# Preparing the ternary weights of an FFN inside the attention that runs before it

## Chip, cores and metric

One core of a Trainium2 chip runs the whole program as one launch. The metric is the device time of that launch in microseconds. The kernel before takes 2642.88 us as the median of three runs (2640.75 to 2642.96).

## What is computed

Two decoder layers over x of 8 batch elements x 256 tokens x 512. Each layer is a gated cross-attention and a gated FFN. The change concerns the first attention (16 heads of 32, with RMS-normed q and k) and the first FFN, a quantised one. Cut to its core:

```python
def activation_quant(x):                      # 8 bits, a scale per token
    s = 127 / clip(max(abs(x), axis=-1, keepdims=True), 1e-5)
    return clip(round(x * s), -128, 127) / s
def weight_quant(w):                          # ternary, one scale per matrix
    s = 1.0 / clip(mean(abs(w)), 1e-5)
    return clip(round(w * s), -1.0, 1.0) / s
def bit_linear(x, w):
    return einsum('bsh,oh->bso', activation_quant(x), weight_quant(w))
# x += tanh(g0) * attention(layernorm(x), context)
# n = layernorm(x);  h = silu(bit_linear(n, w_gate)) * bit_linear(n, w_up)
# x += tanh(g_ffn0) * bit_linear(rms_norm(h) * ln_weight, w_down)
```

Each of the three weight matrices has 512 x 2048 fp32 elements, 8192 on each of 128 partitions (4 MB). The mean of the magnitudes runs over the whole matrix, so no element can be rounded before all of its matrix have been summed.

## The kernel before

The program is written by hand in five parts that run one after another: `image_attention` (tag a), `quantised_ffn` (tag b), `cross_attention`, `latent_attention` and `expert_ffn`. The residual x stays in SBUF all the time as `x_res`, 16 tiles of 128 tokens x 512 fp32, two tiles for each batch element. Within a part every engine has its own instruction list and waits on semaphores; there is no planner.

**The first attention.** The loop runs over turns i from -2 to 7. Turn i finishes batch element i (exponentials, weighting of the values, output projection, addition to x) and starts element i + 1 (values, queries, their norms, transposes, scores) and the keys of i + 2. The order of each engine within a turn is written out: TensorE L592 to L658, ScalarE L739 to L776, VectorE L898 to L948, POOL L440 to L452. ScalarE makes in each turn: the turned peaks (`peaks`, L672), the high half of the turned x (`x_high`), exponentials of four groups of heads, squares of keys and queries with a sum, the high half of the context, high halves of keys and queries, and a copy and a high half of the outputs (`output_raw`, `output_high`). Each fp32 product is made of three products of high and low halves (`split_product`, L45). Products go through a ring of three PSUM banks; `use_of` (L350) numbers their uses in order, and a use waits until the use three before it has been read. `add_to_x` (L878, an addition at L882) is VectorE's last work of a turn. Weights of the attention are held as `w_hi` and `w_lo`, four tensors each; that of the output is `WO`. SP's queue loads x in three transfers (the last is 3 MB, L383) and one context for each turn (L386), the latter once POOL has read the one before (`ctx_lo_done`). `spread` (L791) takes the layer norm's statistics of an element before it is used. POOL begins with memsets (L416 to L420) and selections (L426, L431); ScalarE's first instruction (L730) waits for these.

**The quantised FFN** has a preparation with a block of its own (L976 to L1034). SP loads the three raw matrices (4 MB each), the gate and the layer norm's row. For each matrix ScalarE sums magnitudes (L997), TensorE adds the partitions by a product with ones (L1018), VectorE makes mean and inverse (L1028, L1030), scales and clips in two passes over the 8192 columns (L1032, L1034) and ScalarE rounds to bf16 (L1001). VectorE also takes the statistics of all 16 tiles (L106), aggregates them (L109) and makes an inverse root (L112, L79 to L86). Then a second block holds the FFN proper: its VectorE list begins with the gain product (L1298), which is followed by the norm, the rounding of x and its transposes; the first matmuls are at L1101.

Of the kernel before, what the change touches and what calls it, by code (L numbers as in the profile page):

```python
# [21 lines left out]
P = 128  # L22
# [69 lines left out]
class Norm:  # L92


    def __init__(self, nc, tag, x, begun, place):
        self.x, self.begun = x, begun
        self.stats, self.agg, self.var, self.rstd, self.tmp = (
            place(nc.sbuf_tensor(f"{tag}_ln_{n}", [P, TILES, *shape], F32))
            for n, shape in (("stats", (6,)), ("agg", (2,)), ("var", ()), ("rstd", ()), ("tmp", ())))
        self.stats_done, self.steps = nc.alloc_semaphore(f"{tag}_ln_stats_done"), nc.alloc_semaphore(f"{tag}_ln_steps")  # L100

    def find_spread(self, dve, chain, first, end):

        part = slice(first, end)
        with dve.Fori(first, end) as n:
            dve.bn_stats(self.stats[:, bass.ds(n, 1), :].rearrange("p o n -> p (o n)"), tile_of(self.x, n)).then_inc(self.stats_done, 1)  # L106
        dve.wait_ge(self.stats_done, end)
# [163 lines left out]
def image_attention(nc, x_res, ident, begun, x_in, ctx_t, w_t, rows, gate):  # L271
# [14 lines left out]
    CHAIN = 1 + 9  # L286

    with ExitStack() as ctx:
# [6 lines left out]
        w_hi = [sb(f"w_hi{n}", [P, C, D], F32R) for n in range(4)]  # L295
        w_lo = [sb(f"w_lo{n}", [P, C, D], F32R) for n in range(4)]
# [29 lines left out]
        x_in0, x_in1, x_rest, ctx_in = sem("x_in0"), sem("x_in1"), sem("x_rest"), sem("ctx_in")  # L326
# [24 lines left out]
        for i in TURNS:  # L351
            for name, ahead in PLACES:
                if here(i + ahead) and (name, i + ahead) not in use_of:
                    use_of[name, i + ahead] = len(use_of)

# [13 lines left out]
        def _(sp):  # L369
            sp.dma_start(x_res[:, 0:TB, :], x_in[:, 0:TB, :]).then_inc(x_in0, 16)  # L370
# [8 lines left out]
            sp.dma_start(x_res[:, TB:2 * TB, :], x_in[:, TB:2 * TB, :]).then_inc(x_in1, 16)  # L379
# [3 lines left out]
            sp.dma_start(x_res[:, 2 * TB:, :], x_in[:, 2 * TB:, :]).then_inc(x_rest, 16)  # L383
            for s in range(1, BATCH):
                sp.wait_ge(ctx_lo_done, s)
                sp.dma_start(ctx_f[:, :, :], ctx_t[s]).then_inc(ctx_in, 16)  # L386

        @block.gpsimd
        def _(pool):
# [26 lines left out]
            pool.memset(eps[:, :], RMS_EPS).then_inc(eps_done, 1)  # L416
            pool.memset(neg_peak[:, :, :], 0.0).then_inc(blanked, 1)
# [37 lines left out]
        def _(pe):  # L455
# [130 lines left out]

            pe.wait_ge(begun, 1)
# [2608 lines left out]
```

## Time and profile before

| | before |
|---|---|
| median of 3 runs (lowest, highest) | 2642.88 us (2640.75, 2642.96) |
| the profiled execution: its time, its span | 2643.05 us, 2641.3 us |
| TensorE matmul busy (share of the span) | 2247.1 us (85%) |
| VectorE busy | 1411.7 us (53%) |
| ScalarE busy | 957.3 us (36%) |
| POOL busy | 826.5 us (31%) |
| DMA | 166.46 MB, mean 63 GB/s |

The span is the time from the first to the last recorded instruction of the profiled execution; its own time, 1.75 us longer, is what stands beside the median. Busy times are averages over five parts with different limits, so a stretch has to be read by itself. "PEclk" is the granted clock of TensorE as a share of 2.4 GHz. In the timelines the number in brackets is the idle time of the engine before an instruction, and behind the arrow stands what ended it. A line is that of the kernel before.

### The profile page before, as it was taken

To read this page: it belongs to the slowest core of one execution; us is meant where nothing else is said; L and a number is where in the kernel's file an instruction comes from. 1 tells how busy PE (TensorE), PEld (TensorE's weight loads), DVE (VectorE), ACT (ScalarE), POOL (GpSimd) and SP (SyncE) were. 2 spreads that over 40 slices of the span, in tenths; PEclk is the share of its full clock that TensorE was granted. 3 is DMA by queue.
4 is the path that set the end of the run, shared out by engine and by line. 5 is a ranking of instruction groups with operands and counts; after the bars stand their busy time and mean duration, and the time that the engine had idled before them with its cause. 6 is when DMAs were issued, how large, how long until landed. Compare 5 with 4: busy or idle time off the path is not lost. (4 is left out here: it accounts for less than half of the span.)

```text
span 2641.3 us, 44093 instructions
## 1 busy us (share of the span) xinstructions
PE 2247.1 (85%) x17154; PEld 1824.4 (69%) x17154; DVE 1411.7 (53%) x2430; ACT 957.3 (36%) x1683; POOL 826.5 (31%) x736
## 2 busy tenths in 40 slices
PE   6989984277756999899989998999679999689995
PEld 4666663133325998799879997999556676579995
DVE  7787774677774333433343334333354444567776
ACT  2333332755533222322232222222244544325552
POOL 3332422033322232223222231222343544114543
PEclk8999997699987999999999998999879999899998
DMA  4000003100004001100110011100100000226775
GB/s 175 17 9 9 9 1 135 72 1 0 0 0 176 32 32 64 65 32 32 64 65 32 32 64 62 35 32 32 47 1 2 1 2 2 89 90 246 281 263 215
DMA packets 35814, 166.46 MB, mean 63 GB/s; under 512 B 5712, under 2 KB 5712, under 8 KB 29392
## 3 DMA queue, kind: packets, MB, share of 16 engines
q1 hardware_dynamic: 28624, 141.23, 14.3%
q0 software_dynamic: 7040, 23.07, 2.5%
q8 instruction: 113, 1.85, 0.3%
q14 instruction: 37, 0.30, 0.0%
HBM read 140.17 MB, written 24.12 MB: 62 GB/s over the span
## 5 line engine op out<-in xcount | busy, mean ns | idle before, releaser
L220 POOL TENSOR_TENSOR c_prob<-c_prob,c_inv_mass 128x512 f32<-128x512 f32 x128 | 130.4, 1040 | 392.7 <-DVE c_inv_mass L212 392.7
L202 ACT ACTIVATE c_prob<-c_s_ps,c_neg_peak 128x256 f32<-128x256 f32 x256 | 117.8, 472 | 343.8 <-DVE c_neg_peak L191 343.8
L47 PE MATMUL c_ring<-c_xt_lo,c_w_hi 128*128 128x256 f32 x512 | 149.4, 292 | 21.4 <-DVE c_w_lo L1641 18.7
L1485 POOL TENSOR_TENSOR c_ctx_lo<-c_ctx_f,c_ctx_hi 128x1024 fp32r<-128x1024 f32 x33 | 80.4, 2437 | 271.4 <-ACT c_ctx_hi L1590 271.4
L1074 POOL TENSOR_TENSOR b_hw<-b_h,b_lnw 128x512 f32<-128x512 f32 x64 | 80.1, 1272 | 251.2 <-DVE b_h L1236 251.2
L47 PE MATMUL c_ring<-c_ctx_lo,c_w_hi 128*128 128x256 f32 x512 | 146.6, 286 | 2.1 <-DVE c_qt L1637 2.1
L49 PE MATMUL c_ring<-c_xt_hi,c_w_lo 128*128 128x256 f32 x512 | 143.9, 281 | 0.0
L49 PE MATMUL c_ring<-c_ctx_hi,c_w_lo 128*128 128x256 f32 x512 | 143.8, 281 | 0.0
L48 PE MATMUL c_ring<-c_xt_hi,c_w_hi 128*128 128x256 f32 x512 | 143.7, 281 | 0.0
L48 PE MATMUL c_ring<-c_ctx_hi,c_w_hi 128*128 128x256 f32 x512 | 143.6, 280 | 0.0
L1481 POOL TENSOR_TENSOR c_xt_lo<-c_xt_f,c_xt_hi 128x1024 fp32r<-128x1024 f32 x33 | 84.6, 2564 | 153.7 <-ACT c_xt_hi L1584 153.7
L176 PE MATMUL c_s_ps<-c_kt,c_qt 128*128 128x256 f32 x512 | 121.9, 381 | 8.5 <-ACT c_prob L202 4.8
L259 PE MATMUL c_o_ps<-c_prob_t,c_v 128*128 128x256 f32 x512 | 124.9, 400 | 4.4 <-DVE c_prob_t L247 4.4
L409 POOL TENSOR_TENSOR a_fold<-a_prob 128x1024 f32<-128x1024 f32 x32 | 76.2, 2383 | 147.5 <-ACT a_prob L715 145.8
L1682 DVE SCALAR_TENSOR_TENSOR x_res<-c_ring,c_gain,x_res 128x512 f32 (+1 forms) x64 | 48.1, 751 | 132.2 <-PE c_ring L49 132.2
L259 PEld LDWEIGHTS c_o_ps<-c_prob_t,c_v 128*128 128x128 f32 x512 | 103.1, 202 | 22.1 <-DVE c_prob_t L247 5.4
L47 PE MATMUL c_ring<-c_w_lo,c_o_hi 128*128 128x512 f32 x256 | 104.5, 408 | 10.3 <-DVE c_o_lo L268 7.9
L47 PEld LDWEIGHTS c_ring<-c_xt_lo,c_w_hi 128*128 128x128 f32 x512 | 96.7, 189 | 23.6 <-issue 20.3
L268 DVE TENSOR_TENSOR c_o_lo<-c_o_ps,c_o_hi 128x1024 fp32r<-128x1024 f32 x32 | 39.2, 1224 | 135.7 <-ACT c_o_hi L264 135.7
L176 PEld LDWEIGHTS c_s_ps<-c_kt,c_qt 128*128 128x128 f32 x512 | 94.0, 189 | 24.9 <-ACT c_prob L202 7.1
L1637 DVE COPY c_kt<-c_ring 128x512 f32<-128x512 f32 x64 | 44.3, 691 | 124.8 <-PE c_ring L49 124.8
L1637 DVE COPY c_qt<-c_ring 128x512 f32<-128x512 f32 x64 | 44.2, 691 | 124.1 <-PE c_ring L49 124.1
(514 smaller groups left out, 7119.3 us busy)
## 6 DMA issues: line engine op xcount, KB each, us to landing
e_raw<-e_w SPq DMA_DIRECT2D x16, 1536.0 KB, 6.4
c_xt_f<-xnt_scratch SPq DMA_DIRECT2D x33, 512.0 KB, 3.3
c_ctx_f<-ctx_t SPq DMA_DIRECT2D x33, 512.0 KB, 3.4
c_raw<-c_w SPq DMA_DIRECT2D x16, 1024.0 KB, 6.2
b_raw<-b_w SPq DMA_DIRECT2D x3, 4096.0 KB, 22.5
h_res<-e_w SPq DMA_DIRECT2D x8, 1536.0 KB
h_res<-pairs_scratch SPq DMA_DIRECT2D x10, 512.0 KB, 8.2
a_ctx_f<-ctx_t SPq DMA_DIRECT2D x8, 512.0 KB, 3.4
```

Source lines behind the costliest of these rows:

```text
L47: pe.matmul(out, lhs[0], rhs[1], start=first, stop=False)
L48: pe.matmul(out, lhs[0], rhs[0], start=False, stop=False)
L49: return pe.matmul(out, lhs[1], rhs[0], start=False, stop=last)
L176: mm = pe.matmul(self.s_ps[:, j, 0:w], q_of(u, j), k_of(u, j)[:, 0:w], start=mask is None, stop=True, skip_group_check=mask is not None)
L202: ins = act.activation(self.prob[:, u % 2, j, 0:w], self.s_ps[:, j, 0:w], ACT.Exp, bias=self.neg_peak[:, u % 2, j:j + 1], scale=self.scale ...
L220: pool.tensor_tensor(part, part, self.inv_mass[:, u % 2, js].unsqueeze(2).to_broadcast([P, 2, w]), ALU.mult).then_inc(self.prob_done, 1)
L259: mm = pe.matmul(out_of(g, j), v_of(g, j, t), self.prob_t[:, buf, t, j, :], start=(t == 0), stop=(t == TB - 1))
L409: pool.tensor_tensor(fold[:, n % 2], prob[:, n % 2, :, 0, :], prob[:, n % 2, :, 1, :], ALU.add).then_inc(fold_done, 1)
L1074: pool.tensor_tensor(hw[:, par, cols], h[:, par, cols], lnw[:, cols], ALU.mult).then_inc(hw_done, 1)
L1481: pool.tensor_tensor(xt_lo[:, :, :], xt_f[:, :, :], f32(xt_hi[:, :, :]), ALU.subtract).then_inc(xt_lo_done, 1)
L1485: pool.tensor_tensor(ctx_lo[:, :, :], ctx_f[:, :, :], f32(ctx_hi[:, :, :]), ALU.subtract).then_inc(ctx_lo_done, 1)
L1637: dve.tensor_copy(to, ring[:, k % 2, :]).then_inc(ring_free, count)
```

## The change

The three matrices are made ternary in the first attention. They come in pieces of 128 x 1024 fp32, eight for each matrix, 24 in all, twice: the 24 first steps sum magnitudes (one activation with a sum each), the 24 others round (Identity with the scale 1/mean and a shift of 12582912, then Sign of that less the shift, to bf16). Both are ScalarE's. The pieces lie in the tiles of x of elements 4 to 7, which are loaded later; rounded pieces are stored to DRAM and come back in three 2 MB loads into the place of the attention's q, k and v weights once their last product has been made. The number of steps at each of five places of ScalarE's turn is written out. The mean of all three matrices is one product and three VectorE instructions in turn 1. The layer norm statistics of the FFN are taken in the attention, one element per turn, one turn later, and the preparation block goes. Its DMAs of gate and row, Tanh, the bf16 identity, the aggregation and the root move to the head of the FFN proper.

```diff
 class Norm:
+        self.stats = stats if self.given else place(nc.sbuf_tensor(f"{tag}_ln_stats", [P, TILES, 6], F32))
     def find_spread(self, dve, chain, first, end):
-        with dve.Fori(first, end) as n:
-            dve.bn_stats(...)
-        dve.wait_ge(self.stats_done, end)
+        if not self.given:
+            with dve.Fori(first, end) as n:
+                dve.bn_stats(...)
+            dve.wait_ge(self.stats_done, end)
+PER_WEIGHT = 8
+class Handed:
+    def __init__(self, nc, ctx, w_dram):
+        self.wq = ctx.enter_context(nc.sbuf_tensor("ab_wq", [P, 3 * 2 * C * D], F32R))
+        self.w_mean = ctx.enter_context(nc.sbuf_tensor("ab_w_mean", [P, 3], F32))
+        self.stats = ctx.enter_context(nc.sbuf_tensor("ab_stats", [P, TILES, 6], F32))
+        self.w_dram = w_dram
+        self.wq_dram = nc.dram_tensor("wq_scratch", (3, P, PER_WEIGHT * 1024), BF16, kind="Internal").ap()
 def image_attention(...)
+    PIECE = 1024
+    PIECES = 3 * PER_WEIGHT
+    PLACES_OF_STEPS = {-1: (0, 2, 1, 1, 2), 0: (2, 4, 2, 4, 6), 1: (1, 2, 1, 3, 4), 2: (1, 2, 1, 2, 3), 3: (0, 1, 0, 1, 2)}
+        w_hi = [handed_part(2 * n) for n in range(3)] + [sb("w_hi3", [P, C, D], F32R)]
+        w_lo = [handed_part(2 * n + 1) for n in range(3)] + [sb("w_lo3", [P, C, D], F32R)]
         for i in TURNS:
+            if i == 1:
+                use_of["mean", 0] = len(use_of)
+        for i, n in STEPS.items():
+            for p in range(n):
+                r = p % 4 if i < 2 else (1 + p % 3 if i == 2 else 2 + p % 2)
+                buffer_of.append(r)
...
         @block.sync
-            sp.dma_start(x_res[:, 2 * TB:, :], x_in[:, 2 * TB:, :]).then_inc(x_rest, 16)
-            for s in range(1, BATCH):
+            sp.dma_start(x_res[:, 2 * TB:4 * TB, :], x_dram[:, 2 * TB:4 * TB, :]).then_inc(x_rest, 16)
+            def load_context(s):
                 sp.wait_ge(ctx_lo_done, s)
                 sp.dma_start(ctx_f[:, :, :], ctx_t[s]).then_inc(ctx_in, 16)
+            def load_piece(k):
+                r, n = buffer_of[k], k % PIECES
+                earlier = [j for j in range(k) if buffer_of[j] == r]
+                if earlier and earlier[-1] < PIECES:
+                    sp.wait_ge(summed, earlier[-1] + 1)
+                elif earlier:
+                    sp.wait_ge(piece_out[r], 16 * len([j for j in earlier if j >= PIECES]))
+                sp.dma_start(piece(k), handed.w_dram[n // PER_WEIGHT][:, cols]).then_inc(piece_in[r], 16)
+            def store_piece(k):
+                sp.wait_ge(rounded, n + 1)
+                sp.dma_start(handed.wq_dram[n // PER_WEIGHT][:, cols], piece(k).bitcast(BF16)[:, 0:PIECE]).then_inc(piece_out[buffer_of[k]], 16)
+            def load_late_x(s):
+                r = s - 4
+                sp.wait_ge(piece_out[r], 16 * len([j for j in range(PIECES, 2 * PIECES) if buffer_of[j] == r]))
+                sp.dma_start(x_res[:, s * TB:(s + 1) * TB, :], x_dram[:, s * TB:(s + 1) * TB, :]).then_inc(x_in[r], 16)
+            load_context(1)
+            for i in STEPS:
+                first = FIRST_STEP[i]
+                for p in range(STEPS[i]):
+                    k = first + p
+                    if i < 3:
+                        load_piece(k)
+                    if k - PIECES >= 2 and p >= 2:
+                        store_piece(k - 2)
+                    if i == 3:
+                        load_piece(k)
+                    if p == STEPS[i] // 2:
+                        load_context(i + 3)
+                if first + STEPS[i] > PIECES:
+                    store_piece(first + STEPS[i] - 2)
+                    store_piece(first + STEPS[i] - 1)
+                if i in (1, 2):
+                    load_late_x(i + 3)
+            load_late_x(6)
+            load_late_x(7)
+            load_context(7)
+            await_ready(sp, "q1", BATCH - 1)
+            for n in range(3):
+                sp.dma_start(handed.wq[...].bitcast(BF16), handed.wq_dram[n]).then_inc(wq_in, 16)
+            sp.wait_ge(wq_in, 48)
         @block.gpsimd
             pool.memset(eps[:, :], RMS_EPS).then_inc(eps_done, 1)
+            pool.memset(ones[:, :], 1.0)
+            pool.memset(shifts[:, 0:1], ROUND)
+            pool.memset(shifts[:, 1:2], -ROUND).then_inc(consts_done, 1)
         @block.tensor
                 if now:
                     turn_peaks(i)
+                if i == 1:
+                    use("mean", 0, mean)
                 if i >= 0 and nxt:
                     turn_x(i + 1, 0)
         @block.scalar
+            def next_weights(i, place):
+                for k in steps_of(i, place):
+                    await_piece(act, k)
+                    of = piece(k)
+                    if k < PIECES:
+                        if k > 0:
+                            act.wait_ge(summed, k)
+                        act.activation(of, of, ACT.Abs, accum_out=part[:, k:k + 1]).then_inc(summed, 1)
+                    else:
+                        n = k - PIECES
+                        w = n // PER_WEIGHT
+                        if n == 0:
+                            act.wait_ge(mean_steps, 3)
+                        act.activation(of, of, ACT.Identity, bias=shifts[:, 0:1], scale=inv_mean[:, w:w + 1]).then_inc(shifted, 1)
+                        act.wait_ge(shifted, n + 1)
+                        act.activation(of.bitcast(BF16)[:, 0:PIECE], of, ACT.Sign, bias=shifts[:, 1:2]).then_inc(rounded, 1)
                 if now:
                     exponentials(i, 0)
+                next_weights(i, 0)
...
                 if i >= -1 and here(i + 2):
                     context_high(i + 2)
+                next_weights(i, 1)
...
                     keys_high(i + 1, 1)
+                next_weights(i, 2)
...
                     output_raw(i, 1)
+                next_weights(i, 3)
                 if now:
                     output_high(i, 1)
+                next_weights(i, 4)
         @block.vector
+            def find_spread_after(i):
+                await_free(dve, "o1", i)
+                for t in range(TB):
+                    dve.bn_stats(handed.stats[:, i * TB + t, :], x_res[:, i * TB + t, :])
                     low("xt", i + 1, 0, xt_lo, xt_hi, xt_hi_done)
+                if i == 1:
+                    mean_magnitudes()
                 if nxt:
                     find_spread(i + 2)
+                if i >= 1:
+                    find_spread_after(i - 1)
+                if nxt:
                     value(i + 1, 0)
...
+            find_spread_after(BATCH - 1)
 def quantised_ffn(...)
-        with ExitStack() as prep:
...
+        @block.sync
+            sp.dma_start(gate_sb[:, :], gate).then_inc(gate_in, 16)
+            sp.dma_start(lnw[:, :], ln_row).then_inc(lnw_in, 16)
         @block.gpsimd
+            pool.wait_ge(lnw_in, 16)
             weight(0, 0)
         @block.scalar
+            act.wait_ge(gate_in, 16)
+            act.activation(gain[:, :], gate_sb[:, :], ACT.Tanh).then_inc(gain_done, 1)
             round_x(0)
         @block.vector
+            dve.tensor_copy(ident_b[:, :], ident[:, :])
+            norm_of.find_spread(dve, Chain(dve, norm_of.steps, begun), 0, TILES)
             chain.turn(0)
+            dve.wait_ge(gain_done, 1)
```

## Rows read from the trace of the kernel before

**Rows 1.** Windows: us, busy PE, PEld, DVE, ACT, POOL (instructions), PEclk, DMA share, GB/s
```profile
113.55:162.76 49.21, 45.09 (x452) 32.08 (x451) 38.69 (x56) 17.48 (x29) 16.95 (x9) 0.97 0.04 12
440.25:502.43 62.18, 1.73 (x6) 1.51 (x6) 40.64 (x58) 42.33 (x10) 0.00 (x0) 0.52 0.52 219
507.20:513.10 5.90, 4.72 (x17) 2.08 (x18) 0.00 (x0) 2.73 (x4) 0.00 (x0) 0.50 0.00 0
```

**Rows 2.** Timeline of VectorE, 438 to 503: start, duration, instruction, idle before
```profile
438.34 0.75 DVE L882 SCALAR_TENSOR_TENSOR x_res<-a_ring,a_gain,x_res 128x512 f32<-128x512 f32 x1 [2.05 <-PE a_ring L49]
440.25 0.17 DVE L1022 MEMSET b_ones<- 128x128 f32 x1 [1.16 <-PEq L3115]
...
440.57 9.59 DVE L106 BATCH_NORM_STATS2 b_ln_stats<-x_res  x16
450.19 1.17 DVE L109 BATCH_NORM_AGGREGATE b_ln_agg<-b_ln_stats 128x2 f32<-128x6 f32 x16
...
453.49 0.17 DVE L86 SCALAR_TENSOR_TENSOR b_ln_rstd<-b_ln_tmp,b_ln_rstd 128x16 f32<-128x16 f32 x1
...
502.43 0.21 DVE L1298 TENSOR_SCALAR b_down_gain<-b_w_mean,b_gain 128x1 f32<-128x1 f32 x1 [7.67 <-PEq L976]
```

**Rows 3.** DMA issues: count, KB each, median us to landing
```profile
b_raw<-b_w SPq DMA_DIRECT2D x3, 4096.0 KB, 22.5
...
h_res<-pairs_scratch SPq DMA_DIRECT2D x10, 512.0 KB, 8.2
a_ctx_f<-ctx_t SPq DMA_DIRECT2D x8, 512.0 KB, 3.4
...
out<-x_res SPq DMA_DIRECT2D x16, 256.0 KB, 2.4
...
c_gate_sb<-g_xattn SPq DMA_DIRECT2D x1, 0.5 KB, 2.0
```

**Rows 4.** Timeline of ScalarE: turn 1, a table load, two two-operand activations
```profile
120.06 0.60 ACT L682 ACTIVATE a_xt_hi<-a_ring 128x512 fp32r<-128x512 f32 x1 [2.77 <-PE a_ring L466]
120.55 0.62 ACT L698 ACTIVATE a_junk<-a_kf 128x512 bf16<-128x512 f32 x1
...
121.35 0.63 ACT L698 ACTIVATE a_junk<-a_kf 128x512 bf16<-128x512 f32 x1
...
124.11 1.06 ACT L670 ACTIVATE a_ctx_hi<-a_ctx_f 128x1024 fp32r<-128x1024 f32 x1 [0.21 <-PE a_ring L49]
130.57 0.63 ACT L705 ACTIVATE a_junk<-a_qf 128x512 bf16<-128x512 f32 x1 [5.39 <-DVE a_qf L842]
...
142.57 0.60 ACT L690 ACTIVATE a_qt_hi<-a_ring 128x512 fp32r<-128x512 f32 x1 [3.85 <-PE a_ring L466]
...
153.50 0.63 ACT L727 ACTIVATE a_o_hi<-a_o_f 128x512 fp32r<-128x512 f32 x1 [6.53 <-DVE a_o_f L875]
162.76 0.38 ACT L676 ACTIVATE a_peak_t<-a_ring 128x256 fp32r<-128x256 f32 x1 [8.63 <-PE a_ring L507]
...
511.39 1.28 ACT L1163 ACT_TABLE_LOAD   x1 [2.03 <-PE b_g_ps L1101]
...
1896.22 1.52 ACT L2145 ACTIVATE h_res<-x_res,d_shift,d_rstd 128x512 f32<-128x512 f32 x2 [1.43 <-DVE d_ratio L2312]
```

**Rows 5.** Timeline of VectorE, start of turn 1
```profile
113.34 0.75 DVE L882 SCALAR_TENSOR_TENSOR x_res<-a_ring,a_gain,x_res 128x512 f32<-128x512 f32 x1 [0.67 <-PE a_ring L49]
...
118.33 0.69 DVE L842 TENSOR_TENSOR a_v<-a_ring,a_row 128x512 f32<-128x512 f32 x1 [1.54 <-PE a_ring L49]
120.69 0.69 DVE L856 TENSOR_TENSOR a_xt_lo<-a_ring,a_xt_hi 128x512 fp32r<-128x512 f32 x1 [1.67 <-ACT a_xt_hi L682]
```

**Rows 6.** Timeline of ScalarE, start of the kernel
```profile
1.85 1.28 ACT L730 ACT_TABLE_LOAD   x1 [1.85 <-PEq L3108]
7.71 0.63 ACT L730 ACTIVATE a_pick<-a_fold 128x512 fp32r<-128x512 f32 x1 [4.58 <-POOL a_fold L426]
...
31.46 1.06 ACT L670 ACTIVATE a_ctx_hi<-a_ctx_f 128x1024 fp32r<-128x1024 f32 x1 [4.44 <-DMA a_ctx_f<-ctx_t]
```

More of the change, by code:

```diff
@@ L268, in output_low, with image_attention @@
         dve.tensor_tensor(to, of, f32(high), ALU.subtract).then_inc(self.o_lo_done, 1)
-def image_attention(nc, x_res, ident, begun, x_in, ctx_t, w_t, rows, gate):
+def image_attention(nc, x_res, ident, begun, x_dram, ctx_t, w_t, rows, gate, handed):
     tag = "a"
@@ L286, in image_attention @@
     CHAIN = 1 + 9
+    PIECE = 1024
+    PIECES = 3 * PER_WEIGHT
+    PLACES_OF_STEPS = {-1: (0, 2, 1, 1, 2), 0: (2, 4, 2, 4, 6), 1: (1, 2, 1, 3, 4), 2: (1, 2, 1, 2, 3), 3: (0, 1, 0, 1, 2)}
+    STEPS = {i: sum(n) for i, n in PLACES_OF_STEPS.items()}
+    FIRST_STEP = {i: sum(n for j, n in STEPS.items() if j < i) for i in STEPS}
     with ExitStack() as ctx:
@@ L354, in image_attention, with piece, await_piece, steps_of @@
                     use_of[name, i + ahead] = len(use_of)
+        buffer_of, users, later = [], [0] * 4, []
+        for i, n in STEPS.items():
+            for p in range(n):
+                r = p % 4 if i < 2 else (1 + p % 3 if i == 2 else 2 + p % 2)
+                buffer_of.append(r)
+                later.append(users[r])
+                users[r] += 1
+        def piece(k):
+            at = 2 * TB * TB + TB * buffer_of[k]
+            return x_res[:, at:at + TB, :].rearrange("p t d -> p (t d)")
+        def await_piece(eng, k):
+            eng.wait_ge(piece_in[buffer_of[k]], 16 * later[k] + 16)
+        def steps_of(i, place):
+            if i not in STEPS:
+                return range(0)
+            first = FIRST_STEP[i] + sum(PLACES_OF_STEPS[i][:place])
+            return range(first, first + PLACES_OF_STEPS[i][place])
         def bank_of(name, s):
@@ L585, in outputs, with mean @@
                 use(f"o{t}", i, projected(o_hi, o_lo, WO, t))
+            def mean(bank):
+                pe.wait_ge(consts_done, 1)
+                pe.wait_ge(summed, PIECES)
+                return pe.matmul(bank[:, 0:PIECES], ones[:, :], part[:, :], start=True, stop=True)
             pe.wait_ge(begun, 1)
@@ L775, in _ @@
                     output_raw(i, 1)
+                next_weights(i, 3)
+                if now:
                     output_high(i, 1)
+                next_weights(i, 4)
         @block.vector
@@ L948, in _, with quantised_ffn @@
                     add_to_x(i, 1)
-def quantised_ffn(nc, x_res, ident, begun, w_dram, ln_row, gate):
+            find_spread_after(BATCH - 1)
+def quantised_ffn(nc, x_res, ident, begun, handed, ln_row, gate):
     F = 2048
@@ L966, in sem @@
             return nc.alloc_semaphore(f"b_{name}")
-        wq = [sb(f"wq{n}", [P, WEIGHTS // P], BF16) for n in range(3)]
-        w_mean = sb("w_mean", [P, 3])
+        w_mean = handed.w_mean
         gate_sb, gain = sb("gate_sb", [P, 1]), sb("gain", [P, 1])
```

113 lines of the change are left out of this document (42 added, 71 removed).

## Prediction

> **What bounds the kernel now.** I read the busy time by stretch first. A steady turn of the first attention takes 49.2 us; TensorE is busy for 45.1 of them and ScalarE for 17.5 [rows 1]. So TensorE with its waits sets the turn and ScalarE is idle two thirds of it. From 440.25 to 502.43 the second program prepares its weights: 62.2 us in which TensorE works 1.7 and no DMA, VectorE or ScalarE work of any other stage goes on. Everything in it is on the path, because the first matmul of the FFN needs it. Next VectorE's order of time around that stretch [rows 2]: the last addition to x ends at 439.09, the first instruction of the next program comes at 440.25, sixteen statistics take 9.59, sixteen aggregates and the inverse root go from 450.19 to 453.66, and the gain product that opens the FFN proper starts at 502.43. Between 453.66 and 502.43 lies nothing but the weights, which have to land first (4 MB each, 22.5 us median, [rows 3]). The rows that are still needed afterwards are the aggregates and the root, 3.47 us.
>
> **What the change removes.** After the change VectorE leaves the attention 1.3 us later, since the two statistics of the last batch element come behind its last addition (the same instructions are 9.59/16 = 0.6 apart, [rows 2], with 0.1 for the end of the last). The change of programs costs 1.16 as now. Then the bf16 identity (0.1), aggregates and root (3.47): 439.09 + 1.3 + 1.16 + 0.1 + 3.47 = 445.1. The gain product now waits also for Tanh of the gate. Its DMA is SP's first of the stage; a load of that size lands in 2.0 [rows 3], issued near 441.5 with half a us of issue, so 444.0, Tanh 0.2: 1 us before VectorE asks. The ternary weights are in SBUF already: their load waits for the last q projection, which comes within turn 6, and turn 6 ends by 113.6 + 6 x 49.2 = 409. The second of the 4 MB loads landed after 22.5 with 8.4 MB moved, 370 GB/s, so 6.3 MB need 17: 426 at the latest, 13 us ahead, and more by what of turn 6 is left at its issue. If that cover went, up to 17 would stand on the path. The row of the layer norm (1 MB) has some 15 us before POOL reads it. So the FFN proper starts at 445.1 in place of 502.43: **57.3 us less**. A second effect I put at zero: the first matmuls run at a granted clock of 0.50, the 1.2 GHz level, in 507.2 to 513.1 after TensorE's idle time [rows 1]. Now its idle time shrinks by 57; if the clock stayed at 2.4 GHz, the 4.7 busy us of that stretch would take half, 2.4 less. Bounds: a gain of 2.4 or nothing.
>
> **What it adds on ScalarE.** There are 48 steps in turns -1 to 3. Price [rows 4]: a 128x1024 activation from SBUF takes 1.06; two with a sum (512 wide) start 0.80 apart, so a magnitude step of 1024 takes 0.80 + 0.43 = 1.23. A rounding step has Identity with two per-partition operands: two 512 wide with two such operands took 1.52 together, so 0.80 each with 0.08 of overlap, against 0.63 with none, so 1.06 + 0.17 = 1.23, then a wait for itself (0.08) and Sign with one operand (1.15), less overlap: 2.4. In all 24 x 1.23 + 24 x 2.4 = 87 us, set into the places of a turn where ScalarE waits. These five waits, in turn 1: 2.77, 5.39, 3.85, 6.53, 8.63 [rows 4]. Turn 0 has 2, 4, 2, 4, 6 magnitude steps: 2.5, 4.9, 2.5, 4.9, 7.4, all within. Turn 1 has 1, 2, 1, 3, 4 rounding steps: 2.4, 4.8, 2.4, 7.2, 9.6: the last two are over by 0.7 and 1.0. Behind the first stands the high half of the output, then POOL's low half, for which TensorE already waits; behind the second the turned peaks, for which TensorE waits too. Both are paid: **1.7**. Turn 2 (1, 2, 1, 2, 3) and turn 3 (0, 1, 0, 1, 2) fit.
>
> **The ring and the statistics.** In turn 1 the mean's product takes a bank of the ring between the turned peaks and the first turned x. With three banks that x then needs the bank of the last output product, whose addition ends at 113.34 + 0.75 = 114.09 [rows 5], where it now starts at about 113.4: **0.7**, once. VectorE's statistics (1.3 each turn) and the mean's three small steps (0.6, turn 1) stand before the first value tile, where VectorE idles 1.54, and 1.67 before the next [rows 5]: nothing, or 0.3 in each of seven turns if the cover is short (2 us, upper bound).
>
> **SP's queue.** It now holds 24 loads twice, 24 stores, the split x and the contexts in one order. A 512 KB load lands in 3.4, a 256 KB store in 2.4 [rows 3]. In turn 1 a piece's load is issued when the piece three before it is rounded: lead two steps, 4.8, against 0.4 issue + 3.4: on time by 1. In turn 2 x of element 4 comes only after the last store of turn 1, 4 us late into the turn, which VectorE meets 2 us early; 1.3 + 1.6 of the idle times above absorb that. The piece behind it in the queue lands near 5.2 after the last rounding, ScalarE wants it at 4.1 and had 0.4 to spare: **0.8**. Later turns ask for x near 48 us after the buffer is free. Bounds for all of SP's effects: 0 and, if each piece lands as late as the slowest row of that size, 8.2 [rows 3], the rival below.
>
> **The start.** Three more memsets on POOL come before those that ScalarE's first instruction waits for (idle 4.58, released by POOL, [rows 6]); a memset of 128x128, the largest of them, took 0.17 [rows 2], so **0.3** for the three. In turn -1 the second context had waited 4.44 for its DMA behind 3 MB of x [rows 6]; now 2 MB fewer stand ahead, so it comes up to 3 us sooner and the two magnitude steps behind it fall into that time. Net nothing, with 2 us either way.
>
> **Sum.** 57.3 - 1.7 - 0.7 - 0.8 - 0.3 = 53.8 less. The profiled execution took 2643.05 (span 2641.3), the median of the runs is 2642.88; from either it comes to 2589.
>
> **Rivals.** (a) *Pieces come late.* With landings of 8.2 the lead of 4.8 is short by 3.8 and three steps take 8.2 + 0.5 + 2.4 = 11.1 in place of 7.2, 1.3 a step: up to 31 us over 24 rounding steps, of which the waits of the turn hide part. Say 10 to 28 more, 2599 to 2617. For it: two or three buffers only in turns 2 and 3, stores and loads in one order. Against it: DMA engines are 4% busy in these turns [rows 1]. 0.12.
> (b) *The steps are paid in full, slower than before.* A step that starts in a wait holds ScalarE's queue, and exponentials, copies and squares stand behind it. If nothing of the 87 us is hidden the time is 2589 + 87 - 1.7 = 2674. The kernel gets slower from 55 us on, that is where over 63% of the steps' time falls on the path: each place would have to start late by two thirds of its steps. The five waits of turn 1 sum to 27 us against 26.4 of steps, so turn 1 has no reserve, but turns 0, 2 and 3 have. 0.03.
> (c) *Sign needs another activation table than Exp.* No row has a Sign. One table load takes 1.28 where the trace has it [rows 4]; with one before and one after each Sign a rounding step takes 4.97, and against the same five waits turns 1, 2 and 3 run over by 27.5, 17.6 and 1.3, 46.4 in place of 1.7: 2634, still faster. Abs, Copy, Square, Exp and Tanh share a table here, as ScalarE loads one at 1.85 and the next at 511.39 [rows 4, 6]. 0.04.
> The Trainium skill, "ScalarE: Activation LUTs", section "What ACT_TABLE_LOAD costs", speaks against this change more strongly: each switch costs about 2.66 us with its drain. By that price a step would take 7.7 and the sum would come to 2698, slower than before. The same page's section on table sets names relu, copy, identity and abs as present in every set, and not Sign.
> (d) *Better than the sum:* the clock stays up at the FFN's start (2.4) and the small delays are covered by VectorE's waits: 2585 or 2586. 0.10.
>
> **The numbers.** The forecast has 0.71, its own range 2585 to 2594; (a) 0.12, (d) 0.10, (c) 0.04, (b) 0.03. The predicted time is the forecast's, 2589. The range of 8 in 10 takes in (d) and the lower part of (a): 2584 to 2603. About 0.2% (5.3 us) can be told from no change: faster 0.96, within 0.01 (what lies between (c) and (b)), slower 0.03 (b).
>
> **What would show it.** In the new profile: the gain product of the FFN near 502.4 - 53.8 = 448.6; no stretch of over 10 us with TensorE idle but the change of programs; turn 0 as long as before, turn 1 longer by about 2.4, turn 2 by about 0.8, turns 3 to 6 unchanged; ScalarE's waits at its five places nearly gone in turns 0 and 1, and waits "until DMA" there under 1 us; no table load in the attention but the first; the last load of ternary weights landing before 400. I am wrong if turns 1 to 3 grow by over 8 us together, if ScalarE waits for pieces by several us each, or if VectorE at the FFN's start waits for something not in my list.

## The result and the profile after

The changed kernel takes 2597.36 us (median of 4 runs, 2594.69 to 2599.41) against 2642.79 for the kernel before: a ratio of 0.9829 with a 95% interval of 0.9812 to 0.9846, 45 us faster. The forecast was 2589, its range of 8 in 10 2584 to 2603. The sign came out, 45 of the 54 us came out, and so did the mechanism; 8 us did not. The profiled execution is the 2599.41 one, the slowest of the four (span 2597.6). Its first attention opens as before and ends 10 us later; its FFN starts 46.5 us earlier.

VectorE at the change of programs, in the timeline of the changed kernel (start, duration, instruction, idle time before), answers to [rows 2]:

```profile
448.74 0.75 DVE L1023 SCALAR_TENSOR_TENSOR x_res<-a_ring,a_gain,x_res 128x512 f32<-128x512 f32 x1 [2.31 <-PE a_ring L49]
449.53 1.29 DVE L1029 BATCH_NORM_STATS2 ab_stats<-x_res 128x6 f32<-128x512 f32 x2
452.31 0.23 DVE L1403 CAST b_ident_b<-ident 128x128 bf16<-128x128 f32 x1 [1.49 <-PEq L3226]
452.45 1.16 DVE L111 BATCH_NORM_AGGREGATE b_ln_agg<-ab_stats 128x2 f32<-128x6 f32 x16
...
455.74 0.17 DVE L86 SCALAR_TENSOR_TENSOR b_ln_rstd<-b_ln_tmp,b_ln_rstd 128x16 f32<-128x16 f32 x1
455.94 0.21 DVE L1407 TENSOR_SCALAR b_down_gain<-ab_w_mean,b_gain 128x1 f32<-128x1 f32 x1
```

From the end of the last addition (449.49) to the gain product (455.94) is 6.45 us; it was 502.43 - 439.09 = 63.34 [rows 2]. The head alone gives 56.9.

Turns 1, 2 and 3 of the changed attention and the FFN's first matmuls, windows (busy PE, PEld, DVE, ACT, POOL, PEclk, DMA share, GB/s), to be held against the first and third of [rows 1]. A turn runs from the start of the turned peaks on ScalarE to the next:

```profile
113.16:166.27 53.11, 45.57 (x454) 32.33 (x454) 40.26 (x61) 42.55 (x50) 16.95 (x9) 0.97 0.51 167
166.27:218.29 52.02, 47.69 (x450) 34.56 (x450) 39.55 (x57) 38.00 (x48) 16.97 (x9) 0.90 0.51 157
218.29:269.26 50.97, 44.90 (x450) 32.12 (x449) 40.23 (x58) 26.48 (x38) 16.92 (x9) 0.97 0.32 100
460.71:466.61 5.90, 4.70 (x17) 2.12 (x18) 0.00 (x0) 2.73 (x4) 0.00 (x0) 0.50 0.00 0
```

ScalarE is now busy for 42.6 of 53.1 us in turn 1, where it had 17.5 of 49.2. The turns grew though TensorE's own work in turn 1 hardly did (45.57 for 45.09). By the same marks, turn by turn, in us:

| turn | 0 | 1 | 2 | 3 | 4 | 5 | 6 | 7, to the last addition |
|---|---|---|---|---|---|---|---|---|
| before | 51.20 | 49.21 | 48.40 | 49.38 | 49.11 | 49.36 | 47.04 | 33.04 |
| after | 50.96 | 53.11 | 52.02 | 50.97 | 49.33 | 49.27 | 48.61 | 33.02 |

With the first turn 0.15 earlier the attention is 10.4 us longer, where the forecast had 3.5. What holds ScalarE at the joint of turns 1 and 2, in its timeline:

```profile
159.61 1.24 ACT L858 ACTIVATE x_res<-x_res,a_shifts,a_inv_mean 128x1024 f32<-128x1024 f32 x1
160.89 1.15 ACT L860 ACTIVATE x_res<-x_res,a_shifts 128x1024 bf16<-128x1024 f32 x1
163.94 1.24 ACT L858 ACTIVATE x_res<-x_res,a_shifts,a_inv_mean 128x1024 f32<-128x1024 f32 x1 [1.91 <-DMA x_res<-b_w]
165.22 1.15 ACT L860 ACTIVATE x_res<-x_res,a_shifts 128x1024 bf16<-128x1024 f32 x1
166.27 0.36 ACT L791 ACTIVATE a_peak_t<-a_ring 128x256 fp32r<-128x256 f32 x1
...
172.53 1.25 ACT L858 ACTIVATE x_res<-x_res,a_shifts,a_inv_mean 128x1024 f32<-128x1024 f32 x1 [1.69 <-DMA x_res<-b_w]
```

The piece of turn 1's last step comes 1.91 us late, and the turned peaks, for which TensorE waits, stand behind it in ScalarE's queue. One more piece, at 215.96, is late by 1.83. VectorE and TensorE at the same joint, in their timelines:

```profile
171.23 1.29 DVE L936 BATCH_NORM_STATS2 a_stats<-x_res 128x6 f32<-128x512 f32 x2 [3.38 <-DMA x_res<-x]
...
224.23 1.29 DVE L936 BATCH_NORM_STATS2 a_stats<-x_res 128x6 f32<-128x512 f32 x2 [4.37 <-DMA x_res<-x]
```

```profile
166.78 0.59 PE L649 MATMUL a_s_ps<-a_qt_hi,a_kt_lo 32*128 32x256 f32 x4 [2.79 <-ACT a_peak_t L791]
...
169.38 0.63 PE L48 MATMUL a_ring<-ab_wq,a_ctx_hi 128*128 128x512 f32 x1
```

VectorE waits 3.38 and 4.37 us for x of elements 4 and 5. TensorE waits 2.79 us for the peaks. Then its 128x512 matmuls start 0.43 us apart and take 0.63 each; just before the wait they started 0.23 apart and took 0.39. The ten us from the start of turn 2, before and after, in the windows:

```profile
162.76:172.76 10.00, 9.87 (x111) 7.38 (x110) 5.32 (x17) 6.32 (x11) 2.39 (x1) 1.00 0.01 2
```

```profile
166.27:176.27 10.00, 9.49 (x96) 7.34 (x96) 4.05 (x9) 5.88 (x9) 2.38 (x1) 0.66 0.76 254
```

The first is the kernel before, the second the one after: 111 matmuls against 96, granted clock 1.00 against 0.66. The DMA issues of the changed kernel (count, KB each, median us to landing) answer to [rows 3]:

```profile
x_res<-b_w SPq DMA_DIRECT2D x48, 512.0 KB, 4.9
...
wq_scratch<-x_res SPq DMA_DIRECT2D x24, 256.0 KB, 2.7
ab_wq<-wq_scratch SPq DMA_DIRECT2D x3, 2048.0 KB, 12.4
...
x_res<-x SPq DMA_DIRECT2D x6, 512.0 KB, 4.5
```

The forecast took 3.4 for a piece, from the contexts. The 4.9 is the median of both passes together. The rounding steps use the second pass, which is loaded from 111 us on, and the transfers issued between 111 and 262 us have:

```profile
x_res<-b_w SPq DMA_DIRECT2D x24, 512.0 KB, 4.4
```

The late piece of turn 1 is the one issued between 157.7 and 158 us:

```profile
x_res<-b_w SPq DMA_DIRECT2D x1, 512.0 KB, 6.2
```

SP's queue at the joint of turns 1 and 2 (start, duration of the issue), in its timeline:

```profile
166.39 0.32 SPq L460 DMA_DIRECT2D wq_scratch<-x_res  x1
166.75 0.43 SPq L465 DMA_DIRECT2D x_res<-x  x1
167.23 0.45 SPq L454 DMA_DIRECT2D x_res<-b_w  x1
```

SP issues in one order. The x of element 4 stands behind the store of turn 1's last piece, and that store waits for the rounding, which ends at 166.37. The first piece of turn 2 stands behind both. The last step in element 4's own buffer was stored at 159.7 and had landed by 164.7.

### The profile page after: what moved, and what is told of

Its sections match the earlier page's. It is cut to its first block and busy times, and to the rows that moved or that the text cites. A ratio compares the mean times of both kernels' runs of the same rounds, so it can differ in the third digit from the quotient of the medians.

```text
span 2597.6 us, 44191 instructions
## 1 busy us (share of the span) xinstructions
PE 2253.2 (87%) x17150; PEld 1826.7 (70%) x17150; DVE 1382.9 (53%) x2420; ACT 997.0 (38%) x1770; POOL 828.2 (32%) x739
## 5 line engine op out<-in xcount | busy, mean ns | idle before, releaser
L47 PE MATMUL c_ring<-c_xt_lo,c_w_hi 128*128 128x256 f32 x512 | 149.4, 292 | 21.8 <-DVE c_w_lo L1750 19.2
L47 PE MATMUL c_ring<-c_w_lo,c_o_hi 128*128 128x512 f32 x256 | 103.8, 405 | 10.3 <-DVE c_o_lo L284 7.9
```

What stands on the lines that cost most here:

```text
L47: pe.matmul(out, lhs[0], rhs[1], start=first, stop=False)
```

## The experiments

The theory after the first reading: the 7 us by which the attention grew beyond the forecast are a matter of supply, that is of buffers whose cycle (round, store, load) is longer than the ScalarE work it has to cover. Its rival: the steps themselves cost more than priced, through ScalarE's order, the ring and the clock.

**again** is the changed kernel unchanged.

> The changed kernel once more, for the spread between executions. Both theories below explain the growth of turns 1 to 3 (3.9, 3.6 and 1.6 us over before) and expect the same three figures here within 0.3 us. Turn 6 (1.6 longer) and the FFN (2.1 longer) I put down to TensorE's granted clock: if so, they move by 1 to 3 us between two executions; if the fetch of the ternary weights or the new head of the FFN causes them, they repeat within 0.3.

It took 2596.04 us. Its attention ends 2.5 us earlier than in the first profile, its turns 1 to 3 take 51.92, 52.88 and 49.83. The same two pieces are late (0.89 and 3.19 us). TensorE's wait for the peaks is 1.66 us, and the ten us behind it have a granted clock of 1.00. The lateness is a property of the kernel; the fall of the clock is not in every execution. The three turns did not repeat within 0.3 us, as both theories had it. Turn 6 (48.66 for 48.61) and the FFN from the gain product to its last addition (275.33 for 275.05) did, which by the expectation speaks for a cause in the kernel in both, not for a clock that differs between executions.

**no_dma**: the second pass's loads, all stores and the fetch are left out, and the FFN computes on weights of zeros, made by a VectorE memset ahead of it. The steps stay. With the stores gone, x of elements 4 to 7 waits for the rounding of the last step in its buffer.

```diff
 def load_piece(k):
+    if k >= PIECES:
+        return
...
 def store_piece(k):
+    return
...
 def load_late_x(s):
-    sp.wait_ge(piece_out[r], ...)
+    sp.wait_ge(rounded, ...)
...
-            for n in range(3):
-                sp.dma_start(handed.wq[...], handed.wq_dram[n]).then_inc(wq_in, 16)
-            sp.wait_ge(wq_in, 48)
...
+            dve.memset(f32(handed.wq[:, :]), 0.0)
```

> Leaves out the second loads, the stores and the fetch of the ternary weights: ScalarE rounds what its buffers hold, as often and at the same places, and the FFN works on zeros written by one VectorE memset at its head. Theory S (supply: loads and stores of pieces and the late x take longer than their lead): turn 1 is left with the overshoot of two places and the mean, 49.2 + 2.0 to 2.7; turn 2 below 48.9, turn 3 within 0.3 of 49.4; ScalarE waits for no DMA in them. Theory C (ScalarE's 24 rounding steps are themselves too long for the turns): turns 1 to 3 stay at 53.1, 52.0, 51.0. Turn 6: 47.0 if the fetch had lengthened it, anything from 47 to 48.6 if it was the clock.

Turns 1 to 3 in its windows:

```profile
113.12:163.86 50.74, 45.53 (x454) 32.35 (x454) 40.27 (x61) 42.37 (x50) 16.97 (x9) 0.97 0.07 22
163.86:213.21 49.35, 44.68 (x448) 32.19 (x449) 39.28 (x57) 37.89 (x48) 17.00 (x9) 0.97 0.07 22
213.21:262.34 49.13, 45.14 (x452) 32.21 (x451) 39.84 (x58) 26.60 (x36) 16.94 (x9) 0.97 0.10 34
```

ScalarE does the same 42 and 38 us of work. The three turns are 149.2 us, 2.2 over the 147.0 of before and 6.9 under the 156.1 of after: supply holds. VectorE waits for no x in them either. In the other traces with the same rounding (again, stats_back, after_timed and stats_back_timed) the three turns take 154.6 to 157.2, so supply is 5.4 to 8.0 us by the execution taken. Turns 1 and 2 missed the figures expected of them on either side (50.74 for 51.2 to 51.9, 49.35 for under 48.9), and turn 6 took 49.01, longer than with the fetch. The steps' own cost is bounded by turn 1, 1.5 us over before at the same granted clock, where the forecast had 2.4 for overshoot and ring. The whole kernel took 2599.22, since the memset of 10.3 us and its issue stand in the head of the FFN; the head is 19.2 us here.

**no_stores** keeps the loads and leaves out the stores and the fetch, with the same zeros; a load waits only for the rounding of what its buffer held.

```diff
-                    sp.wait_ge(piece_out[r], 16 * len([j for j in earlier if j >= PIECES]))
+                    sp.wait_ge(rounded, earlier[-1] - PIECES + 1)
...
 def store_piece(k):
+    return
```

> Leaves out the stores of rounded pieces and the fetch (the FFN works on zeros), keeps all loads; a buffer is loaded again as soon as its piece is rounded. Theory S with the store's round trip in the chain (2.8 store + 4.9 load + 2.4 step + issue against 4 x 2.4): without the store a cycle is 7.9 and ScalarE waits for no piece in turn 1: turn 1 50.5 to 51.2 as without any DMA. Turn 2 keeps the wait for x of element 4, which still comes after turn 1's last store place in the queue: 50.5 to 52. If landings alone are too long, turn 1 stays at 52 to 53.

No wait of ScalarE in turns 1 and 2 is put down to a DMA. The turns take 51.33, 49.31 and 48.93, together 149.6: the loads alone cost 0.4 over no_dma, the stores and all that goes with them 6.5. The whole took 2598.81. The expectation had turn 2 keep its wait for x and take 50.5 to 52; the edit frees x as in no_dma, it is issued at 159.72, and VectorE does not wait for it. So the run takes away three things at once: the store's own time in a buffer's cycle, the waits of other DMAs behind a store in SP's order, and the traffic of the stores (the second pass's loads have a median of 3.9 us here, 4.4 with stores). It does not weigh them against each other.

An estimate of the first: with stores a buffer's cycle is 2.4 (rounding) + 2.7 (store) + 4.4 (load) and 0.4 to issue each DMA, 10.3 us. Four buffers give a piece every 2.6 us, where ScalarE asks for one every 2.3 to 2.4 in the seven steps at the end of turn 1, so they fall behind little by little. Only the last piece is late, and most of its lateness is its landing in 6.2. The first piece of turn 2 and x of element 4 are late mostly for the second reason: both stand in SP's queue behind the last store of turn 1.

**x4_early** takes x of element 4 ahead, to the ninth step of turn 1 (`p == 8`), and leaves the last three steps three buffers.

```diff
-                r = p % 4 if i < 2 else ...
+                r = 1 + (p - 8) % 3 if i == 1 and p >= 8 else p % 4 if i < 2 else ...
...
+                    if i == 1 and p == 8:
+                        load_late_x(4)
...
-                if i in (1, 2):
+                if i == 2:
```

> Turn 1 leaves the buffer of element 4's x after its fifth step, and that x is loaded at the ninth, not after the last store; nothing else. S: VectorE's wait of 3.4 for x at the start of turn 2 goes, turn 2 falls from 52.0 to 49.5 to 50.5, and the last three steps of turn 1 have three buffers and wait more, turn 1 53.1 to 55. C: turn 2 stays within 0.5 of 52.0. Neither expects a change in turn 3.

A miss. It took 2601.56, turn 1 58.64 and turn 2 52.16. ScalarE, in its timeline at the end of turn 1:

```profile
158.22 1.24 ACT L860 ACTIVATE x_res<-x_res,a_shifts,a_inv_mean 128x1024 f32<-128x1024 f32 x1 [1.35 <-DMA x_res<-b_w]
164.13 1.24 ACT L860 ACTIVATE x_res<-x_res,a_shifts,a_inv_mean 128x1024 f32<-128x1024 f32 x1 [3.48 <-DMA x_res<-b_w]
169.15 1.24 ACT L860 ACTIVATE x_res<-x_res,a_shifts,a_inv_mean 128x1024 f32<-128x1024 f32 x1 [2.60 <-DMA x_res<-b_w]
```

VectorE's wait for x of element 4 is gone, and three waits of together 7.4 us for pieces have taken its place: the buffer was worth more as a buffer. The estimated cycle of 10.3 over three buffers would give 3.4 us a step, but the last three steps start 5.9 and 5.0 apart. SP's queue in that time shows the rest:

```profile
154.47 0.43 SPq L460 DMA_DIRECT2D wq_scratch<-x_res  x1
...
158.91 0.33 SPq L454 DMA_DIRECT2D x_res<-b_w  x1
159.29 0.43 SPq L460 DMA_DIRECT2D wq_scratch<-x_res  x1
164.80 0.33 SPq L454 DMA_DIRECT2D x_res<-b_w  x1
```

The load at 158.91 waits for the store of 154.47, which lands in 4.4. The next store, of a piece that was rounded at 156.88, stands behind that load and is issued only at 159.29; it lands in 5.5, and the load at 164.80 waits for it. So here store and load took turns in the queue and did not overlap.

Turn 2 stayed long at 52.16, with VectorE's wait for x gone. TensorE had waited 8.46 us, and its clock fell to 0.50 at 168.2, within that wait:

```profile
171.48:181.48 10.00, 9.50 (x96) 7.32 (x96) 4.04 (x9) 5.81 (x9) 2.38 (x1) 0.66 0.62 213
```

It is the same 96 matmuls in ten us at 0.66 as after the 2.79 us wait of the changed kernel. TensorE is busy for 47.82 us of this turn, for 44.68 in no_dma with the same products. So here a part of what turn 2 lost is no wait but the clock. In the changed kernel the fall does not show in the length of the turn: **again** kept a clock of 1.00 at that place, and its turn 2 was 52.88, longer than the 52.02 with the fall.

**stats_back** takes the statistics out of the attention again.

```diff
-                if i >= 1:
-                    find_spread_after(i - 1)
...
-            find_spread_after(BATCH - 1)
-        norm_of = Norm(nc, "b", x_res, begun, ctx.enter_context, handed.stats)
+        norm_of = Norm(nc, "b", x_res, begun, ctx.enter_context)
```

> Only the layer norm statistics go back to the head of the FFN. If VectorE's idle time before the first value tile hides them, the attention's turns change by less than 0.3 each and the whole kernel takes 9.6 - 1.3 = 8.3 us longer. If they lie on the path in the turns, turns 1 to 7 are each up to 1.3 shorter, 9 us in all, and the whole comes out even.

The attention ends at 447.89, within the 446.95 to 449.49 of the two executions with the statistics inside: they are covered there. The head takes 14.98 in place of 6.45, 8.5 more. Yet the run took 2594.05, less than either profiled execution of the changed kernel. The cross-attention, which the edit does not touch, took 1102.9 us from the statistics of its norm to its last addition, and 1108.0 to 1112.3 in the traces of before, after, again, no_dma and x4_early; and the FFN proper was 1.5 shorter than in the profiled execution of after. To tell chance from effect both kernels were timed in five rounds, beside a third:

> The changed kernel, timed beside the others: 0.982 to 0.985 of the kernel before, and turns 1 to 3 longer by 7.5 to 9 us together.

> The statistics back at the head of the FFN, timed. Its one profile had a head 8.5 us longer and still a shorter whole, by a cross-attention that took 9 us less of itself. If that was chance, the whole is 7 to 9 us slower than the changed kernel here (0.3%). If something in this layout makes the cross-attention faster each time, the whole is even or faster and its profile shows the cross-attention near 1103 us again (from the first of its statistics to its last addition), the changed kernel 1112.

The changed kernel: 2593.89 (2590.35 to 2594.78), ratio 0.9822 [0.9808, 0.9835]. With the statistics back: 2597.33 (2594.68 to 2600.89), ratio 0.9839 [0.9826, 0.9853]. So the statistics in the attention are worth 3.4 us by the medians, not the 8.5 of the head; the ranges touch (2594.78 and 2594.68) and the two intervals of the ratio overlap, so the size of this effect is loose. In the traces of these two the head is again 8.5 longer (14.98 and 6.45), the FFN proper 1.8 shorter (273.5 and 275.3), the first attention 1.5 and the cross-attention 1.7 shorter. The last two differ as much between executions of one kernel, and the cross-attention (1106.3 against 1108.0) did not come out at the 1103 and 1112 of the first traces; the FFN is taken up below.

**respaced** is made from the theory: shorter runs of steps in turn 1, the last three steps in turn 4, buffers given by a table so that the late x find theirs free, and SP's DMAs in the order of their due times. These are three changes in one run.

```diff
-    PLACES_OF_STEPS = {..., 1: (1, 2, 1, 3, 4), 2: (1, 2, 1, 2, 3), 3: (0, 1, 0, 1, 2)}
+    PLACES_OF_STEPS = {..., 1: (1, 2, 1, 2, 3), 2: (1, 2, 1, 2, 2), 3: (0, 1, 1, 1, 1), 4: (1, 1, 0, 1, 0)}
+    BUFFERS = {..., 1: (0, 1, 2, 3, 0, 1, 2, 3, 1), 2: (2, 3, 1, 2, 3, 1, 2, 3), 3: (2, 3, 2, 3), 4: (3, 3, 3)}
...
-                r = p % 4 if i < 2 else (1 + p % 3 if i == 2 else 2 + p % 2)
+                r = BUFFERS[i][p]
...
+            for _, issue, which in sorted(issues, key=lambda e: e[0]):
+                issue(which)
```

> Rounding steps per place 1,2,1,2,3 / 1,2,1,2,2 / 0,1,1,1,1 / 1,1,0,1,0 in turns 1 to 4 in place of 1,2,1,3,4 / 1,2,1,2,3 / 0,1,0,1,2; each late x's buffer has its last step in a turn's fourth place, and SP issues loads, stores and x in the order of the times at which they come due. Theory S (supply): no wait of ScalarE for a piece above 1 us, VectorE does not wait for x, turns 1 to 4 together within 2 us of the kernel before (196.1), and the whole is 6 to 9 us faster than the changed kernel. Theory C (ScalarE's steps): as many steps are taken, so the sum of turns 1 to 4 stays within 2 us of the changed kernel (205.4).

2589.01 (2586.06 to 2592.47), ratio 0.9809 [0.9795, 0.9822]: 4.9 us less than the changed kernel in the same five rounds, and the fastest of the timed ones. That is less than the 6 to 9 expected, and the ranges overlap (the changed kernel's lowest is 2590.35); the end of the attention, 6.5 us earlier in the two traces, is the firmer figure. Its turns 1 to 4, in the windows:

```profile
113.68:164.66 50.98, 46.47 (x452) 33.32 (x453) 40.06 (x61) 38.01 (x46) 16.96 (x9) 0.93 0.46 154
164.66:213.93 49.27, 44.88 (x452) 31.97 (x451) 39.78 (x58) 35.73 (x44) 16.98 (x9) 0.97 0.48 159
213.93:262.26 48.33, 43.61 (x452) 31.59 (x451) 39.70 (x58) 26.59 (x36) 16.96 (x9) 1.00 0.27 87
262.26:311.63 49.37, 45.10 (x452) 32.51 (x451) 39.80 (x58) 24.42 (x35) 16.96 (x9) 0.97 0.18 60
```

Together they take 197.95 us, against 196.10 before, 205.43 after and 206.35 in the timed trace of the changed kernel. Of its waits for pieces in these four turns one is left, 0.43 us, and VectorE waits for no x. How much of it is the spacing and how much SP's order no run separates.

**idle_nine** and **idle_four** look at something else. From the gain product to the FFN's last addition the changed kernel takes 275.05 us, where the kernel before took 272.94, with the same instructions. All five traces with the short head had 275.05 to 275.42, those with heads of 15 us and more 272.88 to 273.59. Both kernels are respaced with dependent memsets ahead of the FFN's first work.

```diff
+            for n in range(9):
+                dve.memset(idle_sb[:, :], 0.0).then_inc(idle_done, 1)
+                dve.wait_ge(idle_done, n + 1)
```

> The re-spaced kernel with nine dependent memsets of 128x1024 f32 on VectorE at the head of the FFN, and nothing else; the row of 12288 f32 elements took 10.3 us, so each takes about 0.86 and with its wait 1.0: 9 us of idle time for TensorE and nothing more. Theory L (the length of the head alone sets how long the FFN proper takes, whatever fills it): from the gain product to the last addition of the FFN 273.0 to 273.6 us, as in the kernels with a head of 15 to 20 us, in place of 275.5 in the re-spaced kernel. Theory W (it is the statistics in the attention or the real work of the head that makes the difference, not its length): 275.5. The memsets themselves: the kernel is 9 us slower, or 7 under theory L.

> The re-spaced kernel with four such memsets. If a longer idle time of TensorE makes the FFN proper shorter step by step, the FFN proper takes about 274.5 us; if it is a matter of where the FFN stands in time (a phase), any value from 273 to 276 can come, and the result need not lie between those of zero and nine memsets. Kernel 4 us slower than the re-spaced one, give or take 2.

The head grew to 17.2 and 11.2 us. The FFN proper took 274.84 us with nine and 273.88 with four. Neither figure expected for nine (273.0 to 273.6, or 275.5) came out, nor the 274.5 for four. That a longer head makes the FFN shorter is wrong: 17.2 us of head go with 274.8, 15.0 with 273.6, 11.2 with 273.9. But kernels whose head has the same length repeat within 0.4 us: 275.05 to 275.42 five times at 6.45, 273.59 and 273.50 at 14.98, 272.88 and 272.98 at 19.2. So it is a property of the kernel and not chance. The granted clock goes with it in part. The FFN proper in the windows, first before, then after, then idle_nine:

```profile
502.43:775.37 272.94, 206.84 (x1088) 97.58 (x1088) 195.04 (x521) 143.58 (x241) 80.13 (x64) 0.92 0.00 0
```

```profile
455.94:730.99 275.05, 210.15 (x1088) 99.20 (x1088) 195.09 (x520) 143.93 (x241) 79.96 (x64) 0.90 0.00 2
```

```profile
458.16:733.00 274.84, 211.50 (x1088) 99.84 (x1088) 195.16 (x521) 143.71 (x241) 79.89 (x64) 0.89 0.00 0
```

The three kernels with about 273.0 have 0.91 or 0.92, all others 0.89 or 0.90. But the mean clock does not put those others in order: stats_back takes 273.59 and idle_four 273.88 at 0.90, where the changed kernel takes 275.05 at 0.90. So the cause of the 2 us stays open; where in the FFN the low stretches fall may matter, and no run tests it. The runs took 2597.47 and 2587.98; the second was expected 4 us above the re-spaced kernel and came out 1 below. Both attentions ran the re-spaced turns 1 to 4 in 196.2 us, like the kernel before: their turn 1 took 49.35 and 49.34 at a granted clock of 1.00, against 50.98 at 0.93 in respaced's own trace. In these two executions the rounding added nothing to the four turns, though at a slightly better clock: TensorE was busy for 177.7 of their 196.2 us, for 179.0 of 196.1 before.

## Why the prediction was right, and where it was off

The range held the time, and the case that came is the forecast with part of rival (a) in it. The FFN's 2.1 us and turn 6's 1.6, which no rival had, are part of the miss too. Step by step, against the profiled execution (forecast 2589.25 there, measured 2599.41):

**The head of the FFN: right.** 57.3 us forecast, 56.9 found. VectorE's two statistics end 1.33 us after the last addition (1.3 forecast), the change of programs holds it 1.49 (1.16), aggregates and root take the 3.47 copied from [rows 2]. The gate, landing in 2.2 us, and Tanh were covered, as said: the gain product has no wait before it.

**The fetch: right.** It is issued at 387.15 and SP waits 16.9 us for it (17 forecast), so it is in place near 405, 44 us ahead of the last addition, though not before 400 as the prediction's signs had it. Turn 6 grew by 1.57, but it takes 49.01 in no_dma too, which has no fetch, and 46.98 in idle_four, which has it.

**The clock at the FFN's start: right at zero.** The 5.90 us beginning 4.77 after the gain product have 17 matmuls and a granted clock of 0.50, as in [rows 1]. TensorE now sits idle for 12.09 us between the programs, and comes back at the lower level of 1.2 GHz as before.

**The price of a step: right, and rivals (b) and (c) fall.** From ScalarE's groups by line in turns 0 to 3, with the idle time before them and its releaser:

```profile
L858 ACT ACTIVATE x_res<-x_res,a_shifts,a_inv_mean 128x1024 f32<-128x1024 f32 x23 | 28.3, 1232 | 5.4 <-DMA x_res<-b_w 5.4
L860 ACT ACTIVATE x_res<-x_res,a_shifts 128x1024 bf16<-128x1024 f32 x23 | 26.4, 1149 | 0.8
L852 ACT ACTIVATE x_res<-x_res 128x1024 f32<-128x1024 f32 x18 | 19.0, 1057 | 2.4 <-DMA x_res<-b_w 1.3
```

1.23 and 1.15 are the forecast's figures for a rounding step, and in a run two such steps start 2.32 apart (149.77, 152.09) where 2.4 was taken. The activation of a magnitude step takes 1.06, and with the reading of its sum two start 1.25 apart (78.34, 79.59) where 1.23 was taken. No table load stands between Exp and Sign: in every trace of the changed kernel the first one is followed by the next in the FFN. So Sign cost no switch, and 2634 did not come about. Nor did the 2698 by the price in the Trainium skill, "ScalarE: Activation LUTs", "What ACT_TABLE_LOAD costs"; no run here pays a switch on such a step, so none tests that price.

**Overshoot and ring: too high.** 1.7 + 0.7 forecast for turn 1; no_dma, with every step in place, is 1.5 over before. Turn 2, which was to fit, is 0.95 over before in no_dma, though at a clock of 0.97 against 1.00; the three turns together are 2.2 over, for 2.4 forecast. With one step less at each of the last two places turn 1 takes 49.35 (idle_nine), 0.1 over, though at a clock of 1.00 against 0.97, which leaves up to the 1.2 us of TensorE's busy time between the two (45.09 to 43.85) for the ring.

**SP's queue: the term that failed.** The text said a piece's load has "lead two steps, 4.8, against 0.4 issue + 3.4: on time by 1", and priced all of SP's effects at 0.8. The issue came as said: the late piece of turn 1 is issued at 157.73, right behind the rounding of the piece three before it (157.34), and ScalarE is ready for it at 162.03. At 3.4 it would have been on time by 0.9. The 3.4 was the landing of a context with hardly any other transfer around it. Among loads and stores that follow one another the same 512 KB has a median of 4.4 and this piece takes 6.2. The x of element 4 was foreseen late too, at 4 us into the turn and 2 us behind VectorE; it comes at 5.0 and VectorE waits 3.38 for it, which the idle times named did not absorb. In place of 0.8, supply cost 6.9 us in turns 1 to 3 (156.1 - 149.2), of it 6.5 with the stores. The test "I am wrong if turns 1 to 3 grow by over 8 us together" is met at 9.1; in **again** it is 7.6, so it lies at the border. Rival (a) had the right mechanism and, with landings of 8.2, too large a price (10 to 28 beyond the forecast). What neither had is the clock: a wait of 2.79 us on TensorE was followed by ten us at 0.66, with 96 matmuls, where **again** has 107 at 1.00 and the kernel before 111.

**Not in the sum at all:** the FFN proper, 2.1 us longer with a lower granted clock, and 1.6 in turn 6, where 404.40 to 412.00 run at 0.50 (the stretch at this level is 10.2 us long, from 401.8 on; the kernel before has one of 6.8 in its turn 6):

```profile
404.40:412.00 7.60, 6.63 (x36) 5.16 (x36) 2.86 (x2) 0.63 (x1) 1.26 (x1) 0.50 0.00 1
```

Neither has a cause that a run shows. The difference to the forecast is then: attention 6.9, FFN 2.1, head 0.4, all behind the FFN 0.7: 10.1 of 10.2 us. **The start** took 0.15 less, not 0.3 more: ScalarE's first work comes at 9.27 in place of 7.71 [rows 6], 1.6 later, but turn 0 opens at 62.20 for 62.35. That it came out near nothing is luck as much as the cover that was argued; no run tests it.

## What to carry to other kernels

Work put into an engine's waits needs its operands there at the pace of the burst, not of the turn: divide the whole cycle of a buffer (compute, store, load, issues) by the number of buffers and hold that against the duration of one step, with landings taken from transfers in a busy queue. That quotient is a lower bound: a queue that issues in one order adds to it wherever a DMA stands behind one that still waits, as in x4_early, where 3.4 us a step became 5 to 6. So put the DMAs in the order in which they come due, and where the quotient is above the step, shorten the bursts before buffers are taken away. Here both together, with the same 48 steps spread over one more turn and a table of buffers, brought the four rounding turns from 205.4 us back to 198.0, and in two single executions to 196.2, where the kernel before has 196.1.

## What the runs showed of the hardware

TensorE's granted clock fell behind waits much shorter than the change of programs, and not behind all. The length of the wait alone does not decide it. At the joint of turns 1 and 2 its wait for the peaks was 1.66 us (again), 1.96 (after_timed), 2.79 (the first profile) and 8.46 (x4_early); the ten us behind it had 1.00, 1.00, 0.66 and 0.66. At the joint of turns 2 and 3 it was 1.70 (stats_back), 1.76 (after_timed) and 1.91 (again), followed by 0.83, 1.00 and 0.83. At the start of turn 7 it is 0.56 in every trace, and the ten us behind it have 1.00 in the first profile, 0.83 in idle_four and 0.66 in no_dma. At the joints, behind waits of 1.3 us and more, the ten us hold 107, 101 and 96 matmuls at 1.00, 0.83 and 0.66. The row of **again**, to be held against the two above with 96 matmuls:

```profile
164.01:174.01 10.00, 9.49 (x107) 7.23 (x108) 4.15 (x9) 5.87 (x9) 2.39 (x1) 1.00 0.69 238
```

Programs with the same turn differ by 1 to 2 us in one turn (49.35 at 1.00, 50.98 at 0.93), and the FFN proper by 2 us with equal counts of matmuls (0.92 and 0.90). A difference of 2 us between single executions of such kernels is no evidence for an edit; timed in five rounds the ranges of one kernel still span 4 to 6 us.
